# Routing items moved on TensorE, fewer position steps, keys of the cross attentions ahead of the expert blocks, first maxima over two PSUM banks

## The reference

```python
sign_lens = (1 - mask).sum(-1).astype(jnp.float32) - 1.0
loc_x = jnp.mod(ref + off + loc, sign_lens[:, None, None, None])
xg = loc_x / (key_len - 1) * 2.0 - 1.0
ix = ((xg + 1.0) * key_len - 1.0) / 2.0
x0 = jnp.floor(ix)
dx = ix - x0
...
scores = jnp.einsum('bhqd,bhqkd->bhqk', Qh / math.sqrt(HD), sk)
attn = jax.nn.softmax(scores, axis=-1)
```

## Time and profile before

| what | value |
|---|---|
| median of 3 runs | 2030.15 us (2026.91 to 2045.03) |
| profiled execution, its own time | 2025.46 us |
| its span | 2023.7 us |
| PE busy | 1275.5 us (63%) |
| DVE busy | 1031.4 us (51%) |
| ACT busy | 519.5 us (26%) |
| POOL busy | 562.1 us (28%) |

### The profile page before, as it was taken

How to read it: one execution, slowest core, us unless ns; L and a number is a source line. 1 busy time by engine, 2 the same in 40 slices (tenths; PEclk the granted TensorE clock), 3 DMA queues, 4 the chain that set the end, 5 groups by cost and what they waited for, 6 DMA issues and landing times. The chain is left out here.

```text
span 2023.7 us, 26192 instructions
## 1 busy us (share of the span) xinstructions
PE 1275.5 (63%) x9212; PEld 771.5 (38%) x9212; DVE 1031.4 (51%) x2937; ACT 519.5 (26%) x1047; POOL 562.1 (28%) x700
## 2 busy tenths in 40 slices
PE   1478888888966974364353199468838947884220
PEld 1333333333434873363253188223327822221000
DVE  2454464553542325987775545334442333425997
ACT  0123332332322531222121033123414412331000
POOL 6032213222141016221031300620140062004775
PEclk8569787887778995555555599678978957995555
DMA  5910000000003113432240011400001110001333
GB/s 149 396 75 0 1 1 0 1 5 7 1 17 112 58 59 88 100 108 71 59 125 28 21 56 60 130 11 0 11 28 62 62 30 13 0 1 44 110 111 88
DMA packets 73255, 116.48 MB, mean 58 GB/s; under 512 B 11565, under 2 KB 52320, under 8 KB 70624
## 3 DMA queue, kind: packets, MB, share of 16 engines
q1 hardware_dynamic: 60320, 85.24, 13.7%
q0 software_dynamic: 12800, 29.51, 4.9%
HBM read 77.03 MB, written 37.68 MB: 57 GB/s over the span
## 5 line engine op out<-in xcount | busy, mean ns | idle before, releaser
L1658 DVE CUSTOM_DVE_ANT_0 arena<-ps,far 128x512 f32<-128x512 f32 (+3 forms) x256 | 118.3, 488 | 108.2 <-PE ps L1333 106.0
L1248 POOL TENSOR_SCALAR_AFFINE_SELECT arena<-arena 128x260 f32<-128x260 f32 (+1 forms) x128 | 52.5, 422 | 321.4 <-ACT arena L1526 321.4
L808 POOL DMA_INDIRECT arena<-ys_d,slot_i x64 | 61.6, 963 | 274.7 <-DMA ys_d<-arena 207.5
L2476 POOL DMA_INDIRECT arena<-in_w_ud,arena x128 | 123.3, 964 | 40.1 <-issue 37.5
L979 PEld LDWEIGHTS ps<-arena 128*128 128x128 f32 (+1 forms) x1012 | 123.4, 192 | 4.0
L979 PE MATMUL ps<-arena 128*128 128x128 f32 (+1 forms) x1012 | 123.6, 275 | 0.0
L1355 PE MATMUL ps<-arena 32*128 32x128 f32 (+3 forms) x512 | 122.1, 526 | 1.2 <-DVE arena L1677 1.2
L1526 ACT ACTIVATE arena<-ps 128x1024 f32<-128x1024 f32 (+1 forms) x96 | 84.7, 882 | 129.0 <-PE ps L1355 128.7
L2852 PEld LDWEIGHTS ps<-wide,arena 78*128 78x128 bf16 x3840 | 109.8, 104 | 12.7 <-issue 6.5
L2852 PE MATMUL ps<-wide,arena 78*128 78x32 bf16 x3840 | 109.2, 188 | 8.3 <-ACT wide L2969 3.9
L2354 DVE TENSOR_REDUCE arena<-ps 128x6 f32<-128x462 f32 (+1 forms) x96 | 55.9, 583 | 102.3 <-PE ps L2124 102.3
(11 more groups left out here) (502 smaller groups left out, 2657.1 us busy)
## 6 DMA issues: line engine op xcount, KB each, us to landing
arena<-low_d SPq DMA_DIRECT2D x32, 780.0 KB
xs_d<-zrow SPq DMA_DIRECT2D x1, 10240.0 KB, 30.2
ys_d<-zrow SPq DMA_DIRECT2D x1, 10240.0 KB, 55.1
arena<-xs_d SPq DMA_DIRECT2D x69, 128.0 KB, 2.0
ys_d<-arena SPq DMA_DIRECT2D x69, 128.0 KB, 1.7
arena<-in_w SPq DMA_DIRECT2D x2, 1408.0 KB, 8.5
wide<-in_Wfc SPq DMA_DIRECT2D x1, 2048.0 KB, 11.4
wide<-in_Wproj SPq DMA_DIRECT2D x8, 256.0 KB, 6.4
```

Of the source, the lines that this page charges most:

```text
L808: pool.indirect_dma_start(out=yg[:, t % 4, j, :], out_offset=None, in_=ys_d, in_offset=bass.IndirectOffsetOnAxis(ap=slot_i[:, j, t:t + 1], ...
L1658: ins = nc.vector.tensor_tensor_reduce(junk[:, n % 2, 384 * i:384 * i + w], ps[:, n % 2, 384 * i:384 * i + w], far[:, T - w:T], 1.0, 3 * N ...
L2476: pool.indirect_dma_start(out=rows_g[:, t % 4, h, :], out_offset=None, in_=A["w_ud"], in_offset=bass.IndirectOffsetOnAxis(ap=eidi[:, t % 4 ...
```

## The change

In the routing and the sampled attention: the routing items are made for batch b-1 at the end of b's four units instead of b-2 at the start (`turn` at (3, 2), `logits` at (3, 3), `places(b-2)` at (2, 2)); `norms` and `rstd_of` move to g = 0, `normed` behind the scores of g = 1, `take_logits` to the end of g = 3, ACT's `gates` to (0, 2), `pick` to the end of g = 0, `slots` and `scatter` to g = 3. The row buffers of odd and even batches now alternate. `off`, `y` and `pl` use bank 7 and the rest bank 6, and `take` waits for the one engine that emptied the bank. `wrapped` goes from 12 to 8 steps and `positions` from 14 to 12 by writing integers directly and by `scalar_tensor_tensor`. In the causal attention the items stand ahead of `scores(G, 5)`, places, slots and scatter one iteration later. The cross attentions make k, v, the spread keys and `kbd` (`ahead_*`) before or inside the experts of their stage; `norms(1)` and `normed(1)` stand behind the twelve maxima, and these alternate between banks 0 and 5. At the ends of the three attentions `projected(3)` stands ahead of `places(2)`.

```diff
@@ wrapped and positions
-                ch.link(eng.tensor_scalar(pa, o3, rm, None, ALU.mult))
-                ch.link(eng.tensor_copy(pi, pa))
+                ch.link(eng.tensor_scalar(pi, o3, rm, None, ALU.mult))
                 ch.link(eng.tensor_copy(pb_, pi))
-                ch.link(eng.tensor_tensor(pa, pb_, pa, ALU.subtract))
-                ch.link(eng.tensor_scalar(pa, pa, 0.0, None, ALU.is_gt))
+                ch.link(eng.scalar_tensor_tensor(pa, o3, rm, pb_, ALU.mult, ALU.is_lt))
                 ch.link(eng.tensor_tensor(pb_, pb_, pa, ALU.subtract))
-                ch.link(eng.tensor_scalar(pb_, pb_, m, None, ALU.mult))
-                ch.link(eng.tensor_tensor(o3, o3, pb_, ALU.subtract))
+                ch.link(eng.scalar_tensor_tensor(o3, pb_, less, o3, ALU.mult, ALU.add))
...
@@ sampled attention, banks and tensor
-                uses.append((key, 6 + len(uses) % 2))
+                uses.append((key, 7 if key[0] in ("off", "y", "pl") else 6))
...
-                        if (g, t) == (0, 0) and b >= 2:
-                            R_.turn(pe, take, b - 2)
-                        if (g, t) == (0, 3) and b >= 2:
-                            R_.logits(pe, take, b - 2)
...
-                        if (g, t) == (1, 3) and b >= 2:
-                            R_.places(pe, take, b - 2)
-                        if b == 3 and (g, t) == (3, 0):
-                            R_.turn(pe, take, 2)
-                        if b == 3 and (g, t) == (3, 2):
-                            R_.logits(pe, take, 2)
...
+                        if (g, t) == (2, 2) and b >= 2:
+                            R_.places(pe, take, b - 2)
...
+                        if (g, t) == (3, 2) and b:
+                            R_.turn(pe, take, b - 1)
+                        if (g, t) == (3, 3) and b:
+                            R_.logits(pe, take, b - 1)
                 outputs_turned(B - 1)
+                projected(B - 1)
                 R_.places(pe, take, 2)
-                projected(B - 1)
@@ first causal, tensor
-
-                        scores(G, 5)
-                        weighted(6 * G + 4)
                         if G % 4 == 3 and G >= 7:
                             R_.turn(pe, take, G // 4 - 1)
                         if G % 4 == 0 and G >= 8:
                             R_.logits(pe, take, G // 4 - 2)
-                        if G % 4 == 1 and G >= 9:
+                        if G % 4 == 2 and G >= 10:
                             R_.places(pe, take, G // 4 - 2)
+
+                        scores(G, 5)
+                        weighted(6 * G + 4)
@@ expert_stage
                 def _(pe):
+                    if parts.ahead_tensor is not None:
+                        parts.ahead_tensor(pe)
                     blocks.tensor(pe)
                     parts.tensor(pe)
@@ cross_attention
+            max_bank = lambda n: 5 if n < 12 and n % 2 else 0
...
-                        if n:
+                        if n >= 13:
                             pe.wait_ge(c["max"], n)
-                        nc.tensor.matmul(ps[:, 0, 0:(h1 - h0) * S2], qr[:, b % 2, P * t:P * t + P],
+                        elif n >= 2:
...
                 norms(0)
...
                 normed(0)
+                maxima(0, 0, 12)
+                maximum_out(0)
                 norms(1)
...
-                maxima(0, 0, 6)
                 normed(1)
-                maxima(0, 6, 12)
-                maximum_out(0)
                 maximum_in(0)
```

264 lines of the change are left out of this document (130 added, 134 removed).

## The result

The changed kernel takes 1949.99 us (median of 4 runs, 1944.65 to 1958.89), against 2037.59 (4 runs, 2026.91 to 2051.66) for the kernel before: a ratio of 0.957, 95% interval 0.9494 to 0.9647. The forecast was 1962 in 1946 to 1990. The profiled executions stand at 1958.89 and 2025.46, 66.6 us apart, where the sum had 64.8. The two comparisons differ by some 20 us: the medians are 87.6 us apart. The profile of before is faster than all four of its runs here, 12.1 us under their median, and the profile of after is the slowest of its four, 8.9 us above theirs. That difference is one subject of what follows. One profiled execution further down, that of experiment 9, was 1.8% slower than that kernel's fastest run, and is read for its causal attention alone.

What follows compares the result with a forecast made beforehand. The sampled attention was taken as bound by DVE plus PE's late stops, the causal by PE, cross starts by a chain through all engines. Savings of 64.8 us from 2025.46 gave 1960.7, forecast as 1962, range 1946 to 1990.

Steps and rivals of the forecast that it cites:

- the sum: All stages together: 64.8 us saved, from -51 sampled, -2 causal, -12.3 cross attentions and +0.5 for moved work.
- I take all 44.65 off: Sampled attention: six routing stops of 37.15 us and the 7.5 us wait for POOL's rstd_of all vanish.
- -1.7 and +3.5 of returns: Sampled attention: 1.7 us saved at unit 8; 3.5 us given back by later transposes, gates(1), take_logits(2) and logits(2).
- The stop at `keys_values(3)`: Sampled attention, unit 8: PE waits for DVE's take_logits(0), a stop of about 6.1 us instead of 7.8.
- `gates(1)` was to cost 1.3: Sampled attention, batch 3: ACT's gates(1) waits for the end of DVE's unit 11, holding ACT's copies 1.3 us.
- rival (d): Sampled attention: PE goes to the full clock and half of the remaining stops go, 1951 us; chance 0.06.
- 2.1 us a block: Sampled attention, positions: each block shrinks from 11.3 to 9.0 to 9.3 us, 2.1 saved; -7.3 in all.
- -5 and -6: Starts of the first and second cross attention: maximum_in(0) comes 5 and 6 us earlier.
- rival (b): Cross attentions gain nothing: ahead work delays the first expert block and norms(1) uses up the rest, 1982 us; chance 0.08.
- 17 us by themselves: First cross attention's start: two banks and the vanished wait are worth 17 us alone, 5 in the end.
- I count -1.4 there, -0.5 at places, -0.8 at the end: Causal attention: savings at iteration 10's stop, places and end, with +0.7 for the third scatter; -2 us, bounds +6 and -6.
- (c): Causal attention: PE falls to the lower clock, 0.66 instead of 0.80, 90 us more, 2052 us; chance 0.03.

Runs made afterwards that it cites:

- experiment 9: Kernel before with only places, slots and scatter of the causal attention one iteration later: 2058.05 against 2066.32 us, ratio 0.9958.
- experiment 2: Kernel before with only the sampled attention's routing items moved, with its banks, row buffers and end: 2024.94 against 2077.08 us, ratio 0.9773.
- experiment 7: Changed kernel with keys_values(b+1) and ScalarE's first table step at the fourth tile instead of the second: 1950.07 us, ratio 0.957 to the kernel before.
- experiment 1: Kernel before with only the shorter wrapped and positions, 20 instead of 26 steps: 2065.67 against 2077.08 us, ratio 0.9957.
- experiment 3: Kernel before with only the cross attentions' part of the change, with its end: 2044.34 against 2077.08 us, ratio 0.9858.
- experiment 4: Kernel before with only the causal attention's new order: 2055.06 against 2077.08 us, ratio 0.9898.
- experiment 5: Changed kernel with the first twelve maxima in one bank again: 1974.09 us, ratio 0.9683 to the kernel before.
- experiment 6: Changed kernel with norms(1) behind the fourth and normed(1) behind the eighth of the twelve first maxima: 1942.91 us, ratio 0.9547 to the kernel before.
- experiment 8: The kernel before once more, without edit, for a second trace: one run, 2041.28 us.

## Why the prediction was right, and where it was not

**Routing items.** The step "I take all 44.65 off", with -1.7 and +3.5 of returns, was right: the waits of the scores should be near 25 us and are 25.2, the distance from unit 8 to 15 near 107 and is 105.8. Shown by experiment 2. The stop at `keys_values(3)` was foreseen at 6.1 and is 5.53, and experiment 7 shows what makes it. Units 0 to 8 stay 2.8 us behind the forecast: the stop at unit 7 was to grow by 1.2 and grew by 2.0, `take_logits(0)`, now in unit 7, is three steps of 0.6 us together, and in unit 5 two steps of DVE are 1.5 us longer than their like elsewhere, beside two steps of POOL (L2759, from 897.41 and 901.83). That POOL slows them is the obvious reading (in unit 6 of both profiles the second of them takes 2.44 us, beside another step of POOL), but no run tests it.

```profile
897.75 0.98 DVE L3076 TENSOR_TENSOR arena<-arena 128x160 f32<-128x160 f32 x1
...
902.39 2.33 DVE L3090 TENSOR_TENSOR wide<-wide,arena 128x1280 f32<-128x1280 f32 x1
```

In unit 4 of the same profile they take 0.33 and 1.49. `gates(1)` was to cost 1.3 and the stop at unit 12 is 0.9. That units 8 to 15 fell so exactly rests on a clock of 0.52 and 0.53 in both, so that rival (d), the full clock here, had no part: PE was busy 165.24 of 347 us instead of 163.89 of 395 and the clock did not follow. The Trainium skill ("TensorE: Matmul & The Clock Gate", the part on the HAM clock gate) says that the throttled clock is the default and that activity releases it; the traces show little of such a release in this stretch, with means of 0.52 and 0.53. A slip of the prediction changes no sum: the 11.68 us from 872.98 to 884.66 are unit 3 to unit 4.

**Positions.** 2.1 us a block was forecast and 2.1 was measured in units 0, 4 and 8 (experiment 1). The fused step at 128x320 was taken at 0.49 to 0.53 and costs 0.49 or 0.55, by where its scalar comes from.

**Cross attentions.** Right in mechanism, with -6 and -8.5 instead of -5 and -6 at their starts (experiment 3 beside 1, 2 and 4), and -5.3 and -6.1 in the pair of profiles before and after. The chain itself was put too long: 21.75 us from the first maximum to `maximum_in(0)` were forecast, 18.5 and 20.0 measured, since a maximum cost 0.58 and not 0.73. Against that, the maxima were to begin 7.05 us earlier and began 4.2 earlier in the profile of after, and in experiments 5, 6 and 7 a further 2.3 to 3.0 us earlier; in the profile of after the experts' matmuls ended 2.5 to 3.0 us later behind the scatter than in these (106.3 us against 103.3 to 103.8). The moved work cost 0.1 to 0.2 us: in this stage the first transposes of the experts' rows come 4.4 to 4.5 us after the scatter's end in all traces of the new order and 4.2 to 4.4 in the old. So rival (b) is out. The "17 us by themselves" of the prediction is not the sum of its terms, which is 15.7 (4.25, 2.8 and twelve times 0.72). Measured were 8.2 and 6.6 for the two banks (experiment 5) and 4.1 and 6.3 for the earlier start in the pair of profiles. That most of it would be used up by norms(1) holds, and experiment 6 gets 3.6 and 4.3 back.

**Causal attention: the step that failed.** "I count -1.4 there, -0.5 at places, -0.8 at the end": -2, bounds -6 to +6. Measured: 14 to 20 us (experiment 4 against 1, 2 and 3), outside the bounds. The mechanism, POOL's scatter beside the selects of iteration 10, was right as the cause of the 5.98 us stop, and its length is what I priced. That price, -1.4, was even right for the waiting: PE's idle time in iterations 10 to 12 fell by 1.4 us. What I left out, a term put at nothing, is PE's work around and after the stop at the lower clock: its busy time in these three iterations fell by 12.8 us, with the mean clock at 0.75 before and 0.88 after. Over all traces, the last scatter began at 620.8 us on average in the five with the old order (614.1 to 625.4) and at 605.7 in the seven with the new one (600.9 to 610.3). I had put the clock of this stage as a rival in the other direction only (c). In the profile pair the failing step looks smaller, -8.1, because that execution of before happened to be 6 to 11 us shorter here than the other four. Two signs that the prediction had set for this stage failed too: the clock was to stay at 0.80 and is 0.84, and the 529 us were to stay within 6 and are 520.

**Why the sum came out.** 64.8 forecast and 66.6 in the profiled pair, but not by being right in every term, and so near a hit is luck: that profiled execution of before was faster than any of its other runs (2025.46 against 2026.91 to 2051.66), that of after the slowest of its own. The one of before had the end of cross attention 1 at the higher clock, 7 us, and the 10 us of the causal attention. Of the pair of medians, 87.6 us apart, the sum is short by 23: 12 to 18 of the causal attention and 3.5 of the cross attentions. A further candidate is the main loop of cross attention 1, which the change leaves alone and the sum had at 0: it took 154.2 to 172.7 us in the seven traces with the old cross attention (163.4 on average) and 151.1 to 161.7 in the seven with the new one (155.6). With matmuls of the same number it is the clock that differs; whether the change does it or the draw of the executions is not shown.

The end of cross attention 1 (last `maximum_in` to the end of the scatter) in before, in the kernel before again, and after:

```profile
1474.80:1519.80 45.00, 14.00 (x94) 8.22 (x93) 17.91 (x89) 5.13 (x8) 22.28 (x24) 0.64 0.08 31
```

```profile
1490.00:1541.80 51.80, 21.18 (x94) 10.86 (x93) 17.93 (x89) 5.18 (x8) 18.91 (x20) 0.50 0.06 23
```

```profile
1409.40:1460.30 50.90, 28.09 (x111) 15.64 (x111) 19.02 (x95) 8.26 (x14) 19.58 (x21) 0.51 0.08 25
```

The same items in the same order take 45.0 us at a clock of 0.64 or 51.8 at 0.50. Of seven traces with the old cross attention one has the fast form, of seven with the new one also one (experiment 3, 45.3 us). At the lower clock the change takes 0.9 us off by its reordered end (51.8 to 50.9), where 1.3 were forecast; at the higher one nothing is seen (44.9 and 45.3).

## What to carry to other kernels

Where engines pass work round in a relay and the order is written by hand, list for each item who must have finished and what stands behind it on the waiting engine: the cost of an early item is the length of what is queued behind it, and moving it two tiles later took 4.6 of 5.5 us away (experiment 7). When an engine with a variable clock stops, price its next work at the lower clock too (here 12.8 us of busy time, with 1.4 us of waits), and read more than one execution of the kernel before. After removing a wait ask what the next instruction of that engine waits for: if it is the same step by another route, nothing is gained.

## What the runs showed of the hardware

PE's granted clock is not set by the length of the last stop alone: in the causal attention, stops of 1.57 us were followed by the lower clock in the kernel before (at 491.19 and 517.03 us of experiment 8's profile, iterations 11 and 12, means of 0.75) and by the full one after (at 486.66 and 507.22; 0.98 in iteration 12), with the same work. The same stretch of one program also comes at two clocks in two executions: 45.0 us at 0.64 and 51.8 at 0.50, above. The last stage, the product keys, whose code is untouched, took 174.6 to 175.2 us on the chip of experiments 5 to 8 and in the profiles of before and after, and 192.4 to 197.2 on the other two chips; why was not pursued.
